# Attention softmax in parts: exponentials begun with the first row tile's maximum, two tiles scaled ahead of the next rotary product and two behind it

## What is computed

```python
# first layer, one sequence (of x normalised)
q, k, v = ...                      # x @ Wq.T and so on, 16 heads of 128
q, k = _apply_rope(q, cos, sin), _apply_rope(k, cos, sin)
scores = einsum('bthd,bshd->bhts', q, k) * scale
scores = where(causal, scores, -inf)
attn = softmax(scores, axis=-1)
y = einsum('bhts,bshd->bthd', attn, v).reshape(B, T, H * Dh)
return y / 3.0 @ Wo.T
# last layer: q, k, v with biases, the same softmax, attn @ w_o + b_o
```

## Time and profile before

| | |
|---|---|
| median of 3 runs | 1707.98 us |
| lowest and highest | 1707.63 and 1716.46 us |
| profiled execution, whole | 1707.5 us |
| its span | 1705.7 us |
| mean granted TensorE clock | 0.971 of full speed |

### The profile page before, as it was taken

One profiled execution on the slowest core, in us unless ns is written; L12 is line 12 of the kernel. 1 busy time (PEld: TensorE's weight loads), 2 busy tenths in 40 slices (PEclk: granted clock), 3 DMA queues, 4 the chain that ended last, 5 costly groups with the idle time before them and its releaser, 6 DMA issues. The chain is left out here.

```text
span 1705.7 us, 26053 instructions
## 1 busy us (share of the span) xinstructions
PE 1545.0 (91%) x8400; PEld 1214.7 (71%) x8400; DVE 1165.3 (68%) x2492; ACT 925.6 (54%) x2012; POOL 707.5 (41%) x686
## 2 busy tenths in 40 slices
PE   5999888969999888899989989889998897999898
PEld 4777678967787788645635547568887786888787
DVE  5888867657887678899979964436566444665633
ACT  5555556755665556575556532246555444565543
POOL 5999853224212323179729860121222332222222
PEclk9999999989999999999999999889999998999999
DMA  4212222111112112050042000011111212111111
GB/s 124 84 52 77 74 93 68 61 54 35 40 49 90 59 66 87 28 199 1 1 154 72 1 7 1 7 49 49 49 34 58 72 37 69 48 43 43 65 59 47
DMA packets 34333, 98.37 MB, mean 58 GB/s; under 512 B 6388, under 2 KB 11256, under 8 KB 32072
## 3 DMA queue, kind: packets, MB, share of 16 engines
q1 hardware_dynamic: 33064, 90.95, 16.0%
q0 software_dynamic: 1184, 6.37, 1.1%
HBM read 96.12 MB, written 1.18 MB: 57 GB/s over the span
## 5 line engine op out<-in xcount | busy, mean ns | idle before, releaser
L919 POOL TENSOR_TENSOR head_low<-head,head_high 128x512 fp32r<-128x512 f32 x64 | 81.7, 1277 | 461.3 <-ACT head_high L909 460.6
L1883 POOL TENSOR_TENSOR experts_low<-experts,experts_high 128x1536 fp32r<-128x1536 f32 (+3 forms) x56 | 128.3, 2292 | 262.0 <-ACT experts_high L1833 137.7
L1275 ACT ACTIVATE probs<-banks,neg_max 128x512 f32<-128x512 f32 (+3 forms) x256 | 131.4, 526 | 148.7 <-DVE neg_max L1183 148.7
L2422 POOL TENSOR_TENSOR rings<-du,bc_rows 128x512 f32<-128x512 f32 x124 | 155.7, 1277 | 20.1 <-DVE banks L2348 13.3
L2348 DVE TENSOR_TENSOR_SCAN banks<-banks,rings 128x512 f32<-128x512 f32 x128 | 155.9, 1219 | 2.3 <-POOL rings L2422 1.1
L1525 DVE SCALAR_TENSOR_TENSOR hidden<-banks,weight,act_out 128x96 f32<-128x96 f32 (+1 forms) x192 | 62.7, 368 | 123.7 <-ACT act_out L1493 123.2
L2140 PE MATMUL banks<-rings,ident 128*128 128x512 f32 x256 | 126.3, 608 | 16.4 <-DVE rings L2371 16.1
L1493 ACT ACTIVATE act_out<-banks 128x256 f32<-128x256 f32 (+2 forms) x112 | 47.4, 423 | 171.8 <-PE banks L225 171.7
L225 PE MATMUL banks<-experts_high,xnT_high 128*128 128x384 f32 (+1 forms) x384 | 138.6, 361 | 0.5 <-PEq L187 0.5
L225 PE MATMUL banks<-xnT_high,head_high 128*128 128x512 f32 x256 | 109.9, 429 | 29.9 <-POOL head_low L919 23.8
L225 PE MATMUL banks<-experts_low,xnT_high 128*128 128x384 f32 (+1 forms) x384 | 136.9, 356 | 0.0
(11 more groups left out here) (302 smaller groups left out, 4734.8 us busy)
## 6 DMA issues: line engine op xcount, KB each, us to landing
head<-in_heads SPq DMA_DIRECT2D x64, 384.0 KB, 3.0
experts<-in_experts SPq DMA_DIRECT2D x16, 1152.0 KB, 5.1
bc_rows<-bc_rows SPq DMA_DIRECT2D x30, 512.0 KB, 6.3
experts<-in_experts SPq DMA_DIRECT2D x16, 768.0 KB, 4.2
values<-in_values SPq DMA_DIRECT2D x32, 256.0 KB, 3.2
coef<-in_spline_coef POOLq DMA_DIRECT2D x8, 768.0 KB, 4.7
idx<-in_lut_idx SPq DMA_DIRECT2D x16, 134.0 KB, 2.1
x<-in_x SPq DMA_DIRECT2D x2, 512.0 KB, 4.4
```

The source lines that it names most:

```text
L1275: last = nc.scalar.activation(prob_tile(i), score_tile(i), ACT.Exp, bias=neg_max[:, i:i + 1], scale=QK_SCALE, accum_out=row_sum[:, i:i + 1])
L1883: nc.gpsimd.tensor_tensor(parts[gpar][1][:, columns], raw[gpar][:, columns], parts[gpar][0][:, columns].bitcast(FP32), ALU.subtract)\
L2422: nc.gpsimd.tensor_tensor(inflow[:, step % INFLOWS], du[:, c], B_of(n), ALU.mult)\
```

## The change

The softmax is cut at the row tiles. The negated maximum is now computed three times in a head: for tile 3 alone, for tile 2 alone, and for tiles 1 and 0 together. Each computation raises `max_ready`, and ACT waits for it three times, so that its exponential of tile 3 needs only the maximum of tile 3. ACT raises `exp_ready` twice, after tile 2 and after tile 0. DVE takes the reciprocal in two parts of two columns, and scales tiles 3 and 2 before the first half of the next head's sine product and tiles 1 and 0 behind it. `probs_ready` is still raised once, behind the last scaling.

```diff
-    CHAIN_SOFTMAX = 5
+    CHAIN_SOFTMAX = 6
         def softmax(h, chain, next_turned=False):
+            def negate(tiles):
+                chain.wait()
+                nc.vector.tensor_scalar(neg_max[:, tiles], row_max[:, tiles], -QK_SCALE, None, ALU.mult)\
+                  .then_inc(max_ready.sem, 1)
+
+            def scale(n, tiles):
+
+                dve.wait_ge(exp_ready.sem, exp_ready.at(2 * h + n + 1))
+                chain.all(nc.vector.reciprocal(row_inv[:, tiles], row_sum[:, tiles]))
+                for i in (tiles.stop - 1, tiles.start):
+                    last = nc.vector.tensor_scalar(prob_tile(i), prob_tile(i), row_inv[:, i:i + 1], None, ALU.mult)
+                return last
+
             for n, i in enumerate((3, 2, 1, 0)):
                 if n < 3:
 
                     dve.wait_ge(scored.sem, scored.at(3 * h + n + 1))
                 chain.link(nc.vector.reduce_max(row_max[:, i:i + 1], score_tile(i), AXIS.X))
-            chain.wait()
-            nc.vector.tensor_scalar(neg_max[:], row_max[:], -QK_SCALE, None, ALU.mult)\
-              .then_inc(max_ready.sem, 1)
+                if i != 1:
+                    negate(slice(i, i + 1) if i else slice(0, 2))
+            scale(0, slice(2, 4))
             if next_turned:
                 turn(h + 1, 0, chain)
-
-            dve.wait_ge(exp_ready.sem, exp_ready.at(h + 1))
-            chain.all(nc.vector.reciprocal(row_inv[:], row_sum[:]))
-            for i in (3, 2, 1, 0):
-                last = nc.vector.tensor_scalar(prob_tile(i), prob_tile(i), row_inv[:, i:i + 1], None,
-                                               ALU.mult)
-            last.then_inc(probs_ready.sem, 1)
+            scale(1, slice(0, 2)).then_inc(probs_ready.sem, 1)
...
         def exponentials(h):
 
-            act.wait_ge(max_ready.sem, max_ready.at(h + 1))
-            for i in (3, 2, 1, 0):
+            for n, i in enumerate((3, 2, 1, 0)):
+                if n < 3:
+
+                    act.wait_ge(max_ready.sem, max_ready.at(3 * h + n + 1))
                 last = nc.scalar.activation(prob_tile(i), score_tile(i), ACT.Exp, bias=neg_max[:, i:i + 1],
                                             scale=QK_SCALE, accum_out=row_sum[:, i:i + 1])
-            last.then_inc(exp_ready.sem, 1)
+                if i in (2, 0):
+                    last.then_inc(exp_ready.sem, 1)
```

More of the change, by code:

```diff
@@ L1360, in close @@
         for s, n in ((qk_projected, 2 * HEADS), (v_projected, HEADS), (scored, 3 * HEADS), (turned, 3 * HEADS),
-                     (attended, HEADS), (added, HEADS + 1), (qk_ready, HEADS), (max_ready, HEADS), (exp_ready, HEADS),
+                     (attended, HEADS), (added, HEADS + 1), (qk_ready, HEADS), (max_ready, 3 * HEADS), (exp_ready, 2 * HEADS),
                      (probs_ready, HEADS), (v_ready, HEADS), (probsT_ready, 3 * HEADS), (y_ready, HEADS),
```

## The result

The changed kernel takes 1699.3 us, the median of 8 executions (1693.7 to 1702.0), beside 1708.2 for the kernel before (8 executions, 1706.0 to 1716.5). The medians differ by 8.9 us. The ratio is 0.993 with a 95% interval of 0.9912 to 0.9948, that is 9 to 15 us less. 1694 was forecast, with a range of 1685 to 1707. The direction, the range and "over 0.5%" hold; the narrow forecast of 1690 to 1698 (0.47) is missed by 1.3 us. The sum of the terms for the first layer came as forecast (7.8 us, measured 7.5), that for the last came to half (6.2, measured 3.1). Term by term it is worse: two of them have the wrong sign and three are too small, so that the total owes something to luck. That is the subject of what follows.

What follows compares the result with a forecast made beforehand. PE was taken as the engine to watch, with DVE the bound in stage 1's middle heads. Terms 5 + 0 + 2 + 3 + 3.8 + 0.3 = 14 us, so 1708 - 14 = 1694 us, range 1685 to 1707.

Steps and rivals of the forecast that it cites:

- The sum of the terms for the first layer: Stages 1 and 2 (layer 0): 7.8 us gained; the last layer, stages 3 and 4 (layer 3): 6.2.
- What bounds the kernel: All stages: PE is the engine to watch; its 39.4 us of waits for scaled probabilities are the most to gain.
- The new order: Stage 1 middle heads: DVE's waits for scores, projection and exponentials get covered; 0.38 us a head, 5 us.
- The price of 0.8 us: DVE, each head: two more multiplications at 0.29 us each with gap and seam, one more reciprocal with its gap.
- The estimate of 0.34: DVE, each head: by the skill the two multiplications cost 0.34 us and not 0.58, 3 us more gain in stage 1.
- Will instructions get longer: DVE beside POOL: one-column multiplications take 0.15 us; no queueing assumed for the two new ones, else 0.33 more each.
- the slower rival: One-column multiplications queue behind POOL in stage 1 and the last heads: 4 us lost, 1712; chance 0.1.
- Stages 1 and 2, middle heads and heads 14: Middle heads gain 5 us in stage 1, 0 in stage 2; heads 14 of both gain 1.2 together.
- Heads 15: Last heads: 3.8 us gained, 1.2 each in stages 3 and 4; POOL's subtraction may fall between the scalings.
- the rival "more": No seam cost, last heads ahead of POOL's subtraction, TensorE's clock stays up in tails: 22 us, 1686; chance 0.13.
- it passes on only in part: POOL limits stage 1's head pairs: middle heads give 2, tails fall behind POOL's subtraction (-3): 8 us, 1700; chance 0.2.
- The signs named beforehand: Stage 1: PE's wait falls to 0.7 us, period by 0.3 to 0.5; stage 2 unchanged; ACT waits in 3 and 4.

Runs made afterwards that it cites:

- experiment 3: Changed kernel with the last multiplication, of two columns, cut into two of one column each: 1698.4 us, ratio 0.9935 against the kernel before.
- experiments 7 and 8: Two of five additions of POOL's spline left out, in the changed kernel and in the kernel before: 1688.3 and 1720.1 us, one execution each.

## Why the prediction was right, and where it wasn't

**What bounds the kernel.** Right: no gain in the middle heads of stage 2, little in stages 3 and 4, most in stage 1. "DVE is the bound" in stage 1 was right, but only with its queueing counted. Its own work and its short pauses fit under PE's 11.46 us a head, as stage 2 shows; what puts it over is the queueing behind POOL, 2.9 us a pair before and after.

**The new order.** The three waits went as forecast. Idle time of DVE in 37 to 195 us is 1.4 us ahead of the sine product (4.7 before), 0.1 ahead of the maxima (3.2) and 0.4 ahead of the reciprocals (6.2). A head of stage 1 stands idle 0.92 us less and works 0.43 more, which gives the gain of 0.48 where 0.38 was taken: this mechanism is the one forecast. The price of 0.8 us was too high. In stage 4 from the first maximum to the end of the last multiplication it takes 2.33 us (1509.94 to 1512.27) where it took 1.88, so the two multiplications cost 0.45 and not 0.58: 0.15 each for themselves and 0.07 each for gap and seam, for which I had taken 0.12. The estimate of 0.34 worked out from the Trainium skill (VectorE: DVE Perf Modes, The DRAIN you can't avoid) is as near from the other side. The same section adds that a next instruction that isn't held back starts earlier, which I had left out; the overlap of the maxima, 1.68 us for a sum of 1.94, agrees. Its statement that a semaphore costs nothing extra doesn't fit the 0.07.

**Will instructions get longer.** The assumption on which the slower rival hung is settled: one column takes 0.15 us beside POOL, at any place, and two columns wait for it (0.92, 1.53, 1.69 and 2.50 us). The Trainium skill (VectorE: DVE Perf Modes, What auto-detection actually checks) leaves open what a single element is; for a float32 multiplication of one column on SBUF these rows show that it isn't locked out. But experiment 3 shows that the question was put too narrowly. With only the new instructions priced, the old ones (the scalings and the last multiplication) were taken to last as long as before, although they were moved in time against POOL's. In the middle heads of stage 1 that came out well by luck: what queueing a short head lost a long one got, and 2.9 us a pair stayed 2.9. The queueing per head is a term that the sum put at no change without a reason.

**Stages 1 and 2, middle heads and heads 14.** Right in sign, too low in size: 7.2 for 5; 2.6 in head 14 of stage 1 and 0.35 in that of stage 2 for 1.2 together. The first had been 14.1 us long, with scalings of 2.40 us behind POOL. In stages 3 and 4 heads 14 gave 2.8 for 1.8.

**Heads 15: the step that failed**, by 7 us (3.8 forecast, 3.3 lost). It named the collision, gave stage 2 a range of -2.4 to +2, and then took +0.5 of it. The measured loss is 2.2 us, the far end: ACT rounds the second block right behind the exponentials, so POOL's subtraction follows the scalings wherever they go. Stage 1 was called free of it, having no second block, and lost 1.6: there its instructions queued behind the spline, and the last row below is stage 4's scaling behind the second block.

```profile
213.27 1.69 DVE L1179 TENSOR_SCALAR neg_max<-row_max 128x2 f32<-128x2 f32 x1
...
216.33 2.20 DVE L1187 TENSOR_SCALAR probs<-probs,row_inv 128x256 f32<-128x256 f32 x2
...
1607.88 2.73 DVE L1187 TENSOR_SCALAR probs<-probs,row_inv 128x256 f32<-128x256 f32 x2
```

The turn of stage 1 came 1.0 us later by that, and the work behind it lasted 0.6 longer, at a granted clock of 0.75 and not 0.81. In stages 3 and 4 the forecast of 1.2 for the turn was close (1.13), and what was missing is the clock.

**The clock.** I had it as a bonus in the rival "more", with the waits shortened so that it stays up. It worked against the change: the last heads' waits were shortened but not removed, so more work fell into the slow stretch, and in the first heads two short waits became one long one. Together 0.7 + 1.0 + 2.7 = 4.4 us in layer 3, more than half of the 7.7 that its softmax gained in middle heads, heads 14 and up to the last turn; stage 1's last head adds its 0.6.

**Rivals.** The sum of *more than that* doesn't come out of its terms: 14 + 3 + 3.4 + 3 to 5 is 23 to 25, not 22. The first, *it passes on only in part*, has the right total for the medians (1700) and the right place, the tails behind POOL's subtraction, at 3 us less than the sum where it was 7. Its other leg, that middle heads give only 2 since POOL's total limits a pair, is refuted by the 7.2 measured and by experiments 7 and 8. *Slower* is refuted by the 0.15 us. The signs named beforehand came in stage 2 and in the middle heads of 3 and 4 (ACT now waits some 0.6 us for the value product). In stage 1 they came on average: PE waits 0.6 us a head, the period fell by 0.93 in one head and by nothing in the next, and no wait of PE for `head_low` shows. A scaling of over 2 us was named as the sign of the collision, and stands in the rows of stages 2 and 4.

## What to carry to other kernels

When instructions that queue behind another engine move in time, price the collisions of all of them, old ones too, and look for the other engine's long instructions at the new place: here 7 us of a 14 us sum hung on it, and holding POOL back until the last scaling gave 12.7.
After making one engine ready sooner, look at what it now waits for; an exchange worth nothing before gave 7.6 us here.
A wait that is shortened but not removed may still let TensorE's clock fall, and the work that now starts sooner runs inside the slow stretch. Look also at whether a change joins short waits: here one of 1.67 us was followed by the lower clock in nine of fourteen cases, and two of 0.6 and 0.9 never.
Compare single profiles by the stages that the change touches: the parts outside the attention stages took 909 to 920 us in the fourteen profiles here, with no order in it by the softmax.

## What the runs showed of the hardware

- A float32 multiplication of 128x1 in SBUF takes 0.15 us on DVE whether POOL works or not. One of 128x2 takes 0.17 alone and up to 2.50 us beside POOL: the nine longest of the changed kernel end within 0.03 us of the end of POOL's running instruction.
- Scalings queue instruction by instruction: four of them, 1.27 us alone, took 3.62 behind one addition of 1.84 us and three short multiplications of POOL. With less work on POOL the kernel before was 1 us a pair slower, and its queueing 1.0 us a pair longer.
- The same 29 instructions of TensorE take 4.18 us at a granted clock of 1.00 and 6.42 at 0.67. Products that nobody reads, put into the waits of the last heads, kept the clock up in stages 2 to 4: 9 us by medians, 5.3 of them to be seen in these heads.
- The clock fell after a single wait of 1.67 us in nine of fourteen cases, never in ten after about the same waiting in two pieces (0.62 to 0.66 and 0.85 to 0.88 us in nine, 0.40 and 1.05 in one). What decides in those nine isn't settled.
